# A perceiver block with a state-space layer: the skip term of y by ScalarE instead of TensorE, and a sixth product by C on GpSimd in seven of eight steps

## The chip, the cores and the metric

The kernel runs on one core of one Trainium2 chip. The metric is the device time of one execution in microseconds (us), lower is better. The engines are named as in the profile: PE is TensorE's matmul, PEld its weight load, DVE VectorE, ACT ScalarE, POOL GpSimd, SP SyncE.

## The reference

Three layers work on x (16 sequences of 128 tokens of 512 features): cross attention to 2048 context tokens, a state-space (Mamba) block with an MLP, and a mixture of experts. The change lies in the state-space layer alone:

```python
xz = jnp.einsum('bld,ed->ble', Z, in_proj_w)
x, z = jnp.split(xz, 2, axis=-1)
x = jax.nn.silu(_causal_dw_conv(x, conv_w, conv_b))
x_dbl = jnp.einsum('bld,ed->ble', x, x_proj_w)
dt, Bm, Cm = jnp.split(x_dbl, [DTR, DTR + DS], axis=-1)
dt = jax.nn.softplus(jnp.einsum('blr,dr->bld', dt, dt_proj_w) + dt_proj_b)
A = -jnp.exp(A_log)
deltaA = jnp.exp(dt[..., None] * A)
deltaBx = dt[..., None] * Bm[:, :, None, :] * x[..., None]
# over l: h = deltaA * h + deltaBx;  y = sum over the 16 states of h * C
y = ys.transpose(1, 0, 2) + x * D
y = y * jax.nn.silu(z)
return jnp.einsum('bld,ed->ble', y, out_proj_w)
```

The inner width is 1024 (8 chunks of 128 channels on the partitions) and there are 16 states. `x * D` is the skip term.

## The kernel before

The program has three stages, attention, state space (`mamba`) and MLP with experts. Each engine has its own instruction list, written by hand, and semaphores order the engines.

**Steps, pairs, units.** The state space takes 8 steps (`i` = 0 to 7) of two sequences each, 256 tokens. A step has 4 pairs of chunks and for each pair 8 groups of two states: 32 units, `m` = 0 to 31, with `p = m // 8` and `g = m % 8`. All five engines walk over the same units, each at its own place:

- POOL multiplies `dt_u` by B into one of four slots of `drive` (L1009). It waits until PE has summed unit m - 4, which held the slot.
- ACT makes the decay factors, a copy of zeros (L1163) and four `Exp` of 254 elements (L1167), in one of two PSUM slots of `decay`. It waits for the product by C of unit m - 2, or for its scan alone where that product is POOL's.
- DVE scans (L1299), then multiplies by C into `drive` (L1310). For units in `POOL_C`, the scan writes `drive` and POOL does the multiplication (`c_product`, L981) after its own drive of unit m + 2.
- PE adds `drive` into the bank `y_ps` by two matmuls with the identity (L1444), each printed as two records.

**Ends of a pair.** When all 8 units of a pair are summed, DVE multiplies `y_ps` by the gate (`end_pair`, L1261, placed after the scan of the next pair's first unit) and signals `y_ready`. Before, PE then starts the next pair in the same bank with the skip term: two matmuls of the diagonal of D (`d_diag`, made once by POOL) by `u` (L1440).

**The next step in between.** The front work of step i + 1 is spread over the units of step i. PE: `project_heads` (L1341) after units 0 and 2, `project_out` of pair 3 of the step before after unit 3, `turn` after 6, `project_in_x` (L1356) after 8, 9, 10, 12, `project_in_z` (L1356) after 13, 14, 15, 17, 22, 23, 25, 26, `project_x` (L1382) after 16, `project_dt` (L1394) after 18 and 21, `project_out` (L1405) after 27, 29, 31. DVE: `add_heads` (L1221) after units 2 and 4, whose moments POOL's `norm_rstd` takes after its drive of unit 5, and `convolve` (L1235) after 11, 12, 13, 15. ACT: `log` (L1128) after unit 1, `silu_gate` (L1094) after 4, `silu_u` (L1084) after 17, `take_z` (L1089) after 18, 20, 26, 29, `take_dbc` (L1100, L1101, of `project_x`'s result) after 19. `silu_u`, `log` and `silu_gate` need another activation table, so a table load stands before each and before the next `Exp`.

Step numbers, unit numbers and line numbers below are those of this kernel.

Of the kernel before, what the change touches and what calls it, by code (L numbers as in the profile page):

```python
# [10 lines left out]
ALU = mybir.AluOpType  # L11
ACT = mybir.ActivationFunctionType
AX = mybir.AxisListType

P = 128
# [26 lines left out]
def cross_attention(nc, x, wq_t, bq, ctx_t, wk_t, wv_t, bk, bv, bo, q_dram, attn_dram, x_dram, heads, semaphores):  # L42

    batches, width, keys = ctx_t.shape
    chunks = width // P
# [6 lines left out]
    scale = float(hd) ** -0.5  # L52
# [12 lines left out]
    T = group * queries  # L65
    assert q_steps == 4 and x.shape == (batches, queries, width)

    with ExitStack() as ctx:
# [20 lines left out]
        ident = sb("a_ident", [P, P])  # L89
# [42 lines left out]
        attn_ready, attn_stored = sem("attn_ready"), sem("attn_stored")  # L132
# [341 lines left out]
        def run_tensor(pe):  # L474
# [197 lines left out]
                values(batches - 1, tiles - 1)  # L672
                sum_over_keys(batches - 1)

            def attention_done(eng):
                eng.wait_ge(attn_ready, (batches + 1) * chunks)

            return values_last, attention_done

        return run_sync, run_gpsimd, run_scalar, run_vector, run_tensor  # L680


def mamba(nc, x, attn_dram, wo_t, w_in_t, conv_w, conv_b, w_x_t, w_dt_t, dt_b, a_log, d_skip,
          w_out_t, norm_w, x1_dram, zm_dram, semaphores):

    batches, seq, width = x.shape
# [25 lines left out]
    ACT_ROUND, ACT_LOG0, ACT_GATE = (24, 30), 27, 4  # L712
    ACT_FIRST_Z = (0, 1, 2)
    DVE_SUM, DVE_X1, DVE_CONV = 5, (2, 4), (11, 12, 13, 15)
    LATE_GROUPS = 3
    POOL_C, POOL_C_LAST = (10, 11, 12, 16, 19), (9, 12, 26, 28)
    C_BEHIND = 2

    bc_dram = nc.dram_tensor("bc_scratch", (steps, 2 * states, T), F32).ap()
# [1 line left out]
    with ExitStack() as ctx:  # L721
        def sb(name, shape, dt=F32):
            return ctx.enter_context(nc.sbuf_tensor(name, shape, dt))
# [4 lines left out]
        def sem(name):  # L728
            return semaphores.enter_context(nc.semaphore(name))
# [30 lines left out]
        mix = sb("b_mix", [P, group, width])  # L760
        norm_sb = sb("b_norm", [P, width])
        spare = sb("b_spare", [P, group * width])
        d_diag = sb("b_d_diag", [P, inner_chunks, P])
        w_out = sb("b_w_out", [P, inner_chunks, width])
        gate = (gate_even, sb("b_gate_odd", [P, inner_chunks, T]))

# [6 lines left out]
        decay = psum("b_decay", [P, 2, SG * 2 * T])  # L773

        ready = sem("b_ready")
        a_ready, diag_ready = sem("b_a_ready"), sem("b_diag_ready")
        wo_loaded, loaded, out_loaded = sem("b_wo_loaded"), sem("b_loaded"), sem("b_out_loaded")
        x_half_loaded, z_half_loaded = sem("b_x_half_loaded"), sem("b_z_half_loaded")
        attn_loaded, x_loaded = sem("b_attn_loaded"), sem("b_x_loaded")
# [153 lines left out]
        def run_gpsimd(pool, in_last_step):  # L933
# [57 lines left out]

            def front(j, par):
                norm_rstd(j)
                pool.wait_ge(loaded, LOADED)
                pool.wait_ge(x_product, 1)
                pool.tensor_tensor(d_diag[:], ident[:].unsqueeze(1).to_broadcast([P, inner_chunks, P]),
                                   d_sb[:].unsqueeze(2).to_broadcast([P, inner_chunks, P]),
                                   ALU.mult).then_inc(diag_ready, 1)

            def body(i, par, first, last):  # L1000
                j = i + 1
# [34 lines left out]
            run_steps(pool, front, body, lambda: None)  # L1036
            return lambda: weigh_out(steps - 1)

        def run_scalar(act, in_last_step):
            act.wait_ge(ready, 7)  # L1040

            def take_squares(t):
# [82 lines left out]
            def log(j, h):  # L1125

                act.wait_ge(low_ready, j * 2 + h + 1)
                act.activation(e_round[h], e_round[h], ACT.Ln, bias=1.0).then_inc(log_ready, 1)  # L1128

            def front(j, par):  # L1130
                layernorm(j, par)
                take_turned(j)
                act.wait_ge(x_half_loaded, X_HALF_LOADED)
                for n in range(pairs):
                    tap(j, par, n)
                act.wait_ge(loaded, LOADED)
                act.activation(a_neg[:], a_neg[:], ACT.Exp).then_inc(a_ready, 1)
                silu_u(j, par)
                take_z(j, par, 0)
                take_dbc(j, True)  # L1140
                take_t(j, par, 0)
                exp_of_abs(j, 0)
                round_sum(j, 0)
                take_t(j, par, 1)
                log(j, 0)
                exp_of_abs(j, 1)
                round_sum(j, 1)
                act.wait_ge(a_ready, 2)

            def body(i, par, first, last):  # L1150
                j = i + 1
                for m in range(units):
                    p, g = m // groups, m % groups
                    if not first or m >= 2:
                        k, n = (i, m - 2) if m >= 2 else (i - 1, units + m - 2)
                        if n in on_pool(k):
                            act.wait_ge(scanned, k * units + n + 1)
                        else:
                            wait_for_c_product(act, k, n)
                    if m % (units // 2) == 0:  # L1160
                        act.wait_ge(dt_ready, i * 2 + p // 2 + 1)
                    slot = decay[:, m % 2].rearrange("p (q t) -> p q t", t=seq)
                    act.copy(slot[:, :, 0], zeros[:])  # L1163
                    for s in range(SG):
                        for cc in range(2):
                            c, q = 2 * p + cc, (s * 2 + cc) * group
                            ins = act.activation(slot[:, q:q + group, 1:], by_batch(dt[:, par, c, :])[:, :, 1:], ACT.Exp,  # L1167
                                                 scale=a_neg[:, c, g * SG + s:g * SG + s + 1])
                    ins.then_inc(decay_ready, 1)
                    if m == ACT_LOG1:  # L1170
                        log(i, 1)
                    if m == ACT_GATE:
                        silu_gate(i, par)
                    if first:
                        if m in ACT_FIRST_Z:
                            take_z(i, par, 1 + ACT_FIRST_Z.index(m))
                    else:
                        if m == ACT_SQUARES:
                            take_squares(i - 1)
                        if m == ACT_SCALE:  # L1180
                            scale_out(i - 1)
                    if last:
                        in_last_step(m)
                        continue
                    if m == ACT_XN:
                        layernorm(j, 1 - par)
                    if m == ACT_XN_T:
                        take_turned(j)
                    if m in ACT_TAP:
                        tap(j, 1 - par, ACT_TAP.index(m))  # L1190
                    if m == ACT_U:
                        silu_u(j, 1 - par)
                    if m == ACT_DBC:
                        take_dbc(j, False)
                    if m in ACT_ABS:
                        take_t(j, 1 - par, ACT_ABS.index(m))
                    if m in ACT_EXP:
                        exp_of_abs(j, ACT_EXP.index(m))
                    if m in ACT_ROUND:
                        round_sum(j, ACT_ROUND.index(m))  # L1200
                    if m == ACT_LOG0:
                        log(j, 0)
                    if m in ACT_Z:
                        take_z(j, 1 - par, ACT_Z.index(m))
# [120 lines left out]
            run_steps(dve, front, body, lambda: end_pair(steps - 1, 1, pairs - 1))  # L1325
            return lambda: add_input(steps - 1, 1, True)

        def run_tensor(pe, values_last, attention_done):
            pe.sem_inc(summed, 4)
            pe.wait_ge(ready, 7)  # L1330
            pe.wait_ge(wo_loaded, WO_LOADED)
# [78 lines left out]
            def front(j, par):  # L1410
                for b in range(group):
                    project_heads(j, b, True)
                values_last()
                turn(j, par)
                pe.wait_ge(x_half_loaded, X_HALF_LOADED)
                for n in range(pairs):
                    project_in_x(j, n)
                pe.wait_ge(z_half_loaded, Z_HALF_LOADED)
                for cc in range(2):
                    project_in_z(j, 0, cc)  # L1420
                pe.wait_ge(loaded, LOADED)
                project_x(j, par)
                for h in range(2):
                    project_dt(j, h)
                for n in range(1, pairs):
                    for cc in range(2):
                        project_in_z(j, n, cc)
                pe.wait_ge(diag_ready, 1)
                attention_done(pe)

            def body(i, par, first, last):
                j = i + 1
                for m in range(units):
                    p, g = m // groups, m % groups
                    if g == 0:

                        pe.wait_ge(y_ready, i * pairs + p + 1)
                        for cc in range(2):
                            c = 2 * p + cc
                            pe.matmul(y_ps[:, cc * T:(cc + 1) * T], d_diag[:, c], u[:, par, c, :],  # L1440
                                      start=(cc == 0), stop=False, skip_group_check=True)
                    wait_for_c_product(pe, i, m)
                    for s in range(SG):
                        ins = pe.matmul(y_ps[:], ident[:], drive[:, m % 4, s].rearrange("p c t -> p (c t)"),  # L1444
# [586 lines left out]
def perceiver_layer(nc, i, out):  # L2031
# [8 lines left out]
    with ExitStack() as semaphores:  # L2040
# [24 lines left out]
        @block.scalar  # L2065
        def _(act):
            attention[2](act)
            take_last_squares, scale_last = state_space[2](act, lambda m: high_w1(act, m))
            mlp[2](act, take_last_squares, scale_last)

        @block.vector
# [4 lines left out]

        @block.tensor
        def _(pe):
            values_last, attention_done = attention[4](pe)
            project_last_out, sum_added = state_space[4](pe, values_last, attention_done)  # L2080
            mlp[4](pe, project_last_out, sum_added)


# [34 lines left out]
```

## Time and profile before

| | |
|---|---|
| median of 3 runs | 3999.93 us (3994.23 to 4001.72) |
| the profiled execution's own time | 3999.69 us |
| its span, first to last instruction | 3997.6 us |
| state-space steps 0 to 6, all engines together | about 2475 to 3357 us |
| last step | 3357 to 3484 us |
| busy over the span | PE 3833.1 (96%), DVE 2815.2 (70%), ACT 1751.8 (44%), POOL 1285.3 (32%) |
| mean granted TensorE clock | 0.991 |

Shares over the whole span average three stages with different limits. What the change is worth is to be read between 2475 and 3484 us. "Idle before" with an arrow in a row names what the engine waited for.

### The profile page before, as it was taken

The page shows a single profiled execution, that of the slowest core. Times are in us where ns is not written, and L with a number is a line of the kernel's source. Part 1 is how long each engine was busy: PE and PEld are TensorE (multiplying, and loading weights), DVE is VectorE, ACT ScalarE, POOL GpSimd, SP SyncE. Part 2 cuts the span into 40 slices and gives each one's busy share as a digit, 9 for nine tenths or more (in the row PEclk, how much of TensorE's full clock was granted, in tenths as well). Part 3 has the DMA queues.
Part 4 walks back from the last instruction along what each step waited for, and adds up shares of the span by engine and source line. Part 5 has one row for each costly group of instructions (what it writes and reads, how often), then busy time and mean ns, then how long its engine had stood idle before and what let it go on. Part 6 is the DMA issues. An engine that isn't in the chain of part 4 may idle for free.

```text
span 3997.6 us, 83589 instructions
## 1 busy us (share of the span) xinstructions
PE 3833.1 (96%) x34880; PEld 2809.5 (70%) x34880; DVE 2815.2 (70%) x2964; ACT 1751.8 (44%) x3490; POOL 1285.3 (32%) x604
## 2 busy tenths in 40 slices
PE   8999999999999999999999998999999998799998
PEld 6777777777877777777777776555455554388886
DVE  5667667667657667667666756999999999855443
ACT  2324324424414423423433435777777778422221
POOL 1111111111011011011111112888888888821011
PEclk9999999999999999999999998999999999999999
DMA  4110110110110011010011023112211122120000
GB/s 155 38 43 29 39 43 29 39 43 29 38 53 31 29 51 31 29 51 31 29 51 40 33 67 101 33 37 64 59 59 34 42 64 85 37 77 22 32 23 21
DMA packets 96902, 183.73 MB, mean 46 GB/s; under 512 B 8450, under 2 KB 12930, under 8 KB 96547
## 3 DMA queue, kind: packets, MB, share of 16 engines
q1 hardware_dynamic: 96546, 178.27, 13.9%
q8 instruction: 311, 5.10, 0.5%
q14 instruction: 45, 0.36, 0.0%
HBM read 152.82 MB, written 25.43 MB: 45 GB/s over the span
## 4 chain that ended last, share of the span: by engine, by line
PE 78%; DVE 10%; POOL 5%; ACT 3%; issue 3%; DMA 0%; DVEq 0%; POOLq 0%; ACTq 0%; SPq 0%
PE scores L523 31%; PE scores L602 8%; PE o_acc L616 6%; PE b_y L1444 6%; PE c_acc L1961 4%; PE c_ring L1946 4%; DVE max_parts L407 4%; DVE b_decay L1299 3%; PE scores L596 3%; POOL b_drive L1009 2%; PE b_work L1356 2%; PE scores L571 2%; PE b_work L1405 2%; PE c_experts_ps L1993 1%; PE b_work L1341 1%
## 5 line engine op out<-in xcount | busy, mean ns | idle before, releaser
L244 POOL TENSOR_TENSOR c_lo<-c_raw,c_hi 128x2048 fp32r<-128x2048 f32 x64 | 294.9, 4607 | 1974.5 <-DVE c_hi L346 1974.5
L434 DVE TENSOR_TENSOR prob_sums<-prob_sums,probs 128x1024 f32<-128x1024 f32 x480 | 566.7, 1222 | 115.3 <-ACT probs L319 115.3
L1009 POOL TENSOR_TENSOR b_drive<-b_dt_u,b_bc 128x1024 f32<-128x1024 f32 x256 | 600.0, 2357 | 112.8 <-PE b_y L1444 79.0
L407 DVE TENSOR_REDUCE max_parts<-scores 128x2 f32<-128x1024 f32 x512 | 602.0, 1218 | 40.6 <-PE scores L571 40.6
L319 ACT ACTIVATE probs<-scores 128x512 f32<-128x512 f32 x1024 | 528.9, 604 | 215.3 <-PE scores L602 213.8
L399 DVE SCALAR_TENSOR_TENSOR k_lo<-scores,bk_sb,k_hi 128x512 fp32r<-128x512 f32 x256 | 192.3, 751 | 565.5 <-ACT k_hi L304 565.5
L1444 PE MATMUL b_y<-b_drive,b_ident 128*128 128x512 f32 x1024 | 497.0, 615 | 73.2 <-DVE b_drive L1310 51.9
L1299 DVE TENSOR_TENSOR_SCAN b_decay<-b_decay,b_drive 128x1024 f32<-128x1024 f32 x217 | 496.5, 2288 | 12.9 <-ACT b_decay L1167 9.2
L304 ACT ACTIVATE k_hi<-scores,bk_sb 128x512 fp32r<-128x512 f32 x256 | 176.3, 689 | 604.7 <-PE scores L523 604.7
L312 ACT COPY v_sb<-scores 128x512 f32<-128x512 f32 x240 | 140.8, 587 | 669.1 <-PE scores L523 669.1
L1167 ACT ACTIVATE b_decay<-b_dt,b_a 128x254 f32<-128x254 f32 x1024 | 425.1, 461 | 0.4
L1444 PEld LDWEIGHTS b_y<-b_drive,b_ident 128*128 128x128 f32 x1024 | 188.5, 193 | 300.3 <-issue 162.6
L602 PE MATMUL scores<-q_hi,k_lo 32*128 32x128 f32 x4096 | 304.4, 270 | 0.6 <-issue 0.6
L602 PE MATMUL scores<-q_lo,k_hi 32*128 32x128 f32 x4096 | 304.3, 270 | 0.0
L602 PE MATMUL scores<-q_hi,k_hi 32*128 32x128 f32 x4096 | 290.9, 256 | 0.0
L523 PE MATMUL scores<-c_hi,wk_hi 128*128 128x512 f32 x1024 | 287.7, 403 | 0.0
L523 PE MATMUL scores<-wv_hi,c_hi 128*128 128x512 f32 x960 | 281.5, 415 | 0.0
L616 PE MATMUL o_acc<-probs,v_sb 128*32 128x128 f32 x8192 | 277.0, 276 | 0.0
L523 PE MATMUL scores<-c_hi,wk_lo 128*128 128x512 f32 x1024 | 274.9, 390 | 0.0
L523 PE MATMUL scores<-c_lo,wk_hi 128*128 128x512 f32 x1024 | 273.8, 389 | 0.0
L1310 DVE TENSOR_TENSOR b_drive<-b_decay,b_bc 128x1024 f32<-128x1024 f32 x217 | 265.4, 1223 | 6.7
L523 PE MATMUL scores<-wv_lo,c_hi 128*128 128x512 f32 x960 | 258.7, 391 | 0.0
(231 smaller groups left out, 6506.3 us busy)
## 6 DMA issues: line engine op xcount, KB each, us to landing
c_raw<-in_ctx SPq DMA_DIRECT2D x64, 1024.0 KB, 5.2
b_bc<-bc_scratch SPq DMA_DIRECT2D x128, 256.0 KB, 4.3
c_w_raw<-in_mlp_w SPq DMA_DIRECT2D x16, 512.0 KB, 3.6
q_scratch<-v_sb SPq DMA_DIRECT2D x4, 1024.0 KB, 4.3
q_raw<-q_scratch SPq DMA_DIRECT2D x16, 256.0 KB, 5.1
q_raw<-in_x SPq DMA_DIRECT2D x16, 256.0 KB, 2.7
x_scratch<-q_raw SPq DMA_DIRECT2D x16, 256.0 KB, 5.8
attn_scratch<-attn_out_sb SPq DMA_DIRECT2D x16, 256.0 KB, 2.0
```

Source lines behind the costliest of these rows:

```text
L244: pool.tensor_tensor(c_lo[:, slot], c_raw[:], c_hi[:, slot].bitcast(F32), ALU.subtract).then_inc(c_lo_ready, 1)
L319: act.activation(probs[:, (2 * t + j // 2) % 4, j % 2, :], score_bank(t, j), ACT.Exp, scale=scale).then_inc(exp_done, 1)
L407: dve.tensor_reduce(max_parts[:, g, 2 * pair:2 * pair + 2, s], max_banks[:, 2 * pair:2 * pair + 2, :], AX.X, ALU.max).then_inc(max_taken, 1)
L434: dve.tensor_tensor(part, part, probs[:, u % 4], ALU.add).then_inc(summed, 1)
L523: ins = pe.matmul(out, lhs, rhs, start=(m == 0), stop=(m == len(steps) - 1))
L602: ins = pe.matmul(banks[j][:, g * queries:(g + 1) * queries], k_part[head_rows(j), g, ts], q_part[head_rows(j), g, :], start=False, stop=last,
L616: ins = pe.matmul(o_acc[head_rows(j), g * queries:(g + 1) * queries], v_sb[:, t, h * hd:(h + 1) * hd], probs[:, (2 * t + j // 2) % 4, j % ...
L1009: pool.tensor_tensor(drive[:, m % 4], dt_u[:, 2 * p:2 * p + 2, :].unsqueeze(1).to_broadcast([P, SG, 2, T]), bc[:, g, 0].unsqueeze(2).to_br ...
L1167: ins = act.activation(slot[:, q:q + group, 1:], by_batch(dt[:, par, c, :])[:, :, 1:], ACT.Exp, scale=a_neg[:, c, g * SG + s:g * SG + s + 1])
L1299: dve.tensor_tensor_scan(state, decay[:, m % 2], increments, 0.0, ALU.mult, ALU.add).then_inc(scanned, 1)
L1310: dve.tensor_tensor(drive[:, m % 4], decay[:, m % 2].rearrange("p (n c t) -> p n c t", c=2, t=T), bc[:, g, 1].unsqueeze(2).to_broadcast([P ...
L1444: ins = pe.matmul(y_ps[:], ident[:], drive[:, m % 4, s].rearrange("p c t -> p (c t)"), start=False, stop=(g == groups - 1 and s == SG - 1) ...
```

## The change

PE's two matmuls of D's diagonal go, with `d_diag`, its making on POOL and its semaphore. ACT writes `u * D` into `y_ps` itself: `begin_sums`, two activations (`Copy`, scale by a column of D) of 256 elements, ahead of the decay factors of units 2, 10, 19 and 26 (2, 10, 18, 26 in the last step). It waits for `y_ready`, and PE's first sum of a pair waits for it (`y_begun`). The wait for the end of the attention's use of that bank moves from PE to ACT. Unit 14 joins POOL's products by C in steps 0 to 6.

```diff
-    POOL_C, POOL_C_LAST = (10, 11, 12, 16, 19), (9, 12, 26, 28)
+    Y_BEGIN, Y_BEGIN_LAST = (2, 10, 19, 26), (2, 10, 18, 26)
+    POOL_C, POOL_C_LAST = (10, 11, 12, 14, 16, 19), (9, 12, 26, 28)
...
-                pool.wait_ge(loaded, LOADED)
-                pool.wait_ge(x_product, 1)
-                pool.tensor_tensor(d_diag[:], ident[:].unsqueeze(1).to_broadcast([P, inner_chunks, P]),
-                                   d_sb[:].unsqueeze(2).to_broadcast([P, inner_chunks, P]),
-                                   ALU.mult).then_inc(diag_ready, 1)
...
+            def begin_sums(i, par, p):
+
+                act.wait_ge(y_ready, i * pairs + p + 1)
+                for cc in range(2):
+                    c = 2 * p + cc
+                    ins = act.activation(y_ps[:, cc * T:(cc + 1) * T], u[:, par, c, :], ACT.Copy, scale=d_sb[:, c:c + 1])
+                ins.then_inc(y_begun, 1)
...
                     p, g = m // groups, m % groups
+                    if m in (Y_BEGIN_LAST if last else Y_BEGIN):
+                        if first and m == Y_BEGIN[0]:
+                            attention_done(act)
+                        begin_sums(i, par, p)
...
                     if g == 0:
-
-                        pe.wait_ge(y_ready, i * pairs + p + 1)
-                        for cc in range(2):
-                            c = 2 * p + cc
-                            pe.matmul(y_ps[:, cc * T:(cc + 1) * T], d_diag[:, c], u[:, par, c, :],
-                                      start=(cc == 0), stop=False, skip_group_check=True)
+                        pe.wait_ge(y_begun, i * pairs + p + 1)
```

ACT in step 3, from the decay factors of unit 17 to those of unit 19. Before, L1084 is `silu_u`, L1089 `take_z`, L1163 and L1167 the decay factors:

```order
L1167 ACTIVATE b_decay<-b_dt,b_a 128x2x127 x4
L1084 ACT_TABLE_LOAD
L1084 ACTIVATE b_u<-b_u 128x1024 x2
L1163 COPY b_decay<-b_zeros 128x8
L1167 ACT_TABLE_LOAD
L1167 ACTIVATE b_decay<-b_dt,b_a 128x2x127 x4
L1089 COPY b_gate_even<-b_work 128x512
L1163 COPY b_decay<-b_zeros 128x8
L1167 ACTIVATE b_decay<-b_dt,b_a 128x2x127 x4
```

The same place in the changed kernel, where L1079 is `silu_u`, L1084 `take_z`, L1130 `begin_sums`:

```order
L1174 ACTIVATE b_decay<-b_dt,b_a 128x2x127 x4
L1079 ACT_TABLE_LOAD
L1079 ACTIVATE b_u<-b_u 128x1024 x2
L1170 COPY b_decay<-b_zeros 128x8
L1174 ACT_TABLE_LOAD
L1174 ACTIVATE b_decay<-b_dt,b_a 128x2x127 x4
L1084 COPY b_gate_even<-b_work 128x512
L1130 ACTIVATE b_y<-b_u,b_d 128x256 x2
L1170 COPY b_decay<-b_zeros 128x8
L1174 ACTIVATE b_decay<-b_dt,b_a 128x2x127 x4
```

`begin_sums` of pair 2 stands behind both table loads, the factors of unit 18 and `take_z`.

ACT at the start of step 3, from the factors of unit 1 to those of unit 2, in the changed kernel (L1123 is `log`; before, the row of L1130 is not there):

```order
L1174 ACTIVATE b_decay<-b_dt,b_a 128x2x127 x4
L1123 ACT_TABLE_LOAD
L1123 ACTIVATE b_spare<-b_spare 128x1024
L1130 ACTIVATE b_y<-b_u,b_d 128x256 x2
L1170 COPY b_decay<-b_zeros 128x8
L1174 ACT_TABLE_LOAD
L1174 ACTIVATE b_decay<-b_dt,b_a 128x2x127 x4
```

Here it stands between `log` and the factors of unit 2.

POOL in step 3 from the drive of unit 14 to that of unit 21, changed kernel (L1004 makes the drives, L1009 before):

```order
L1004 TENSOR_TENSOR b_drive<-b_dt_u,b_bc 128x1024
L981 TENSOR_TENSOR b_drive<-b_drive,b_bc 128x1024
L1004 TENSOR_TENSOR b_drive<-b_dt_u,b_bc 128x1024 x2
L981 TENSOR_TENSOR b_drive<-b_drive,b_bc 128x1024
L1004 TENSOR_TENSOR b_drive<-b_dt_u,b_bc 128x1024 x2
L981 TENSOR_TENSOR b_drive<-b_drive,b_bc 128x1024
L1004 TENSOR_TENSOR b_drive<-b_dt_u,b_bc 128x1024 x3
```

Before, the four drives of units 15 to 18 stood in one row; the product of unit 14 now splits them after unit 16.

## Rows read from the trace of the kernel before

**Rows 1.** Stretches of step 3: length, then each engine's busy us, PEclk, DMA

```profile
2897.00:2913.00 16.00, 13.92 (x54) 9.60 (x53) 15.79 (x20) 11.77 (x31) 16.00 (x8) 1.00 0.09 34
2913.00:2929.00 16.00, 16.00 (x59) 11.09 (x60) 15.04 (x17) 10.91 (x22) 11.92 (x6) 1.00 0.00 0
2929.00:2955.00 26.00, 26.00 (x85) 14.51 (x84) 23.97 (x15) 20.82 (x48) 21.88 (x10) 1.00 0.01 3
```

**Rows 2.** Timeline of PE, step 3: start, length, operation, count, idle before

```profile
2912.89 1.98 PE L1444 MATMUL b_y<-b_drive,b_ident 128*128 128x512 f32 x4 [2.08 <-POOL b_drive L981]
...
2928.50 1.03 PE L1440 MATMUL b_y<-b_u,b_d_diag 128*128 128x256 f32 x4
2929.36 1.88 PE L1444 MATMUL b_y<-b_drive,b_ident 128*128 128x512 f32 x4
```

**Rows 3.** Timeline of DVE, first scan of steps 2, 3, 4 and 5

```profile
2729.26 2.29 DVE L1299 TENSOR_TENSOR_SCAN b_decay<-b_decay,b_drive 128x1024 f32<-128x1024 f32 x1
...
2856.01 2.30 DVE L1299 TENSOR_TENSOR_SCAN b_decay<-b_decay,b_drive 128x1024 f32<-128x1024 f32 x1
...
2981.17 2.30 DVE L1299 TENSOR_TENSOR_SCAN b_decay<-b_decay,b_drive 128x1024 f32<-128x1024 f32 x1
...
3106.55 2.30 DVE L1299 TENSOR_TENSOR_SCAN b_decay<-b_decay,b_drive 128x1024 f32<-128x1024 f32 x1
```

**Rows 4.** Timeline of DVE, step 3: scans 10, 11, 14, 15 and end_pair

```profile
2896.65 4.46 DVE L1299 TENSOR_TENSOR_SCAN b_drive<-b_decay,b_drive 128x1024 f32<-128x1024 f32 x2
...
2914.40 2.29 DVE L1299 TENSOR_TENSOR_SCAN b_decay<-b_decay,b_drive 128x1024 f32<-128x1024 f32 x1
...
2917.86 2.29 DVE L1299 TENSOR_TENSOR_SCAN b_decay<-b_decay,b_drive 128x1024 f32<-128x1024 f32 x1
...
2926.97 0.69 DVE L1261 TENSOR_TENSOR b_gate_odd<-b_y,b_gate_odd 128x512 f32<-128x512 f32 x1 [0.78 <-PE b_y L1444]
```

**Rows 5.** Timeline of POOL, step 3: product 12, drives 15 to 17

```profile
2910.49 2.35 POOL L981 TENSOR_TENSOR b_drive<-b_drive,b_bc 128x1024 f32<-128x1024 f32 x1
2912.80 4.67 POOL L1009 TENSOR_TENSOR b_drive<-b_dt_u,b_bc 128x1024 f32<-128x1024 f32 x2
2920.13 2.36 POOL L1009 TENSOR_TENSOR b_drive<-b_dt_u,b_bc 128x1024 f32<-128x1024 f32 x1 [2.67 <-PE b_y L1444]
```

**Rows 6.** Timeline of ACT: before unit 10, take_z, two Exp

```profile
2893.30 0.17 ACT L1163 COPY b_decay<-b_zeros 128x8 f32<-128x8 f32 x1 [1.11 <-DVE b_drive L1310]
...
2929.49 0.57 ACT L1089 COPY b_gate_even<-b_work 128x512 f32<-128x512 f32 x1
...
2999.43 0.87 ACT L1167 ACTIVATE b_decay<-b_dt,b_a 128x254 f32<-128x254 f32 x2
```

**Rows 7.** Timeline of step 4: PE's first sum of pair 2, ACT's take_z

```profile
3054.64 1.98 PE L1444 MATMUL b_y<-b_drive,b_ident 128*128 128x512 f32 x4
...
3055.46 0.58 ACT L1089 COPY b_gate_odd<-b_work 128x512 f32<-128x512 f32 x1
```

**Rows 8.** Timeline of the start of step 4: PE, ACT, DVE

```profile
2986.55 1.03 PE L1440 MATMUL b_y<-b_u,b_d_diag 128*128 128x256 f32 x4
...
2985.31 0.16 ACT L1163 COPY b_decay<-b_zeros 128x8 f32<-128x8 f32 x1
...
2986.77 1.66 ACT L1167 ACTIVATE b_decay<-b_dt,b_a 128x254 f32<-128x254 f32 x4
...
2988.56 2.29 DVE L1299 TENSOR_TENSOR_SCAN b_decay<-b_decay,b_drive 128x1024 f32<-128x1024 f32 x1
...
2992.84 0.69 DVE L1221 TENSOR_TENSOR b_x<-b_work,b_x 128x512 f32<-128x512 f32 x1 [0.73 <-PE b_work L1341]
```

**Rows 9.** Stretches around units 5 to 8: steps 3, 2, 4

```profile
2874.00:2897.00 23.00, 18.92 (x55) 9.04 (x54) 22.75 (x20) 14.78 (x40) 18.83 (x15) 1.00 0.06 24
...
2748.00:2771.00 23.00, 19.54 (x47) 9.10 (x46) 20.69 (x19) 13.81 (x37) 19.32 (x15) 0.85 0.06 24
3000.00:3023.00 23.00, 19.54 (x53) 9.24 (x52) 22.05 (x20) 13.98 (x38) 19.67 (x15) 0.93 0.06 23
```

More of the change, by code:

```diff
@@ L673, in values_last, with attention_done @@
                 sum_over_keys(batches - 1)
[L675 to L680, printed above, removed]
+            return values_last
+        def attention_done(eng):
+            eng.wait_ge(attn_ready, (batches + 1) * chunks)
+        return run_sync, run_gpsimd, run_scalar, run_vector, run_tensor, attention_done
 def mamba(nc, x, attn_dram, wo_t, w_in_t, conv_w, conv_b, w_x_t, w_dt_t, dt_b, a_log, d_skip,
@@ L762, in mamba @@
         spare = sb("b_spare", [P, group * width])
-        d_diag = sb("b_d_diag", [P, inner_chunks, P])
         w_out = sb("b_w_out", [P, inner_chunks, width])
@@ L775, in mamba @@
         ready = sem("b_ready")
-        a_ready, diag_ready = sem("b_a_ready"), sem("b_diag_ready")
+        a_ready, y_begun = sem("b_a_ready"), sem("b_y_begun")
         wo_loaded, loaded, out_loaded = sem("b_wo_loaded"), sem("b_loaded"), sem("b_out_loaded")
@@ L1037, in run_gpsimd, with run_scalar @@
             return lambda: weigh_out(steps - 1)
-        def run_scalar(act, in_last_step):
+        def run_scalar(act, in_last_step, attention_done):
             act.wait_ge(ready, 7)
@@ L1326, in run_vector, with run_tensor @@
             return lambda: add_input(steps - 1, 1, True)
-        def run_tensor(pe, values_last, attention_done):
+        def run_tensor(pe, values_last):
             pe.sem_inc(summed, 4)
@@ L1427, in front @@
                         project_in_z(j, n, cc)
-                pe.wait_ge(diag_ready, 1)
-                attention_done(pe)
             def body(i, par, first, last):
@@ L2067, in _ @@
             attention[2](act)
-            take_last_squares, scale_last = state_space[2](act, lambda m: high_w1(act, m))
+            take_last_squares, scale_last = state_space[2](act, lambda m: high_w1(act, m), attention[5])
             mlp[2](act, take_last_squares, scale_last)
@@ L2078, in _ @@
         def _(pe):
-            values_last, attention_done = attention[4](pe)
-            project_last_out, sum_added = state_space[4](pe, values_last, attention_done)
+            values_last = attention[4](pe)
+            project_last_out, sum_added = state_space[4](pe, values_last)
             mlp[4](pe, project_last_out, sum_added)
```

## The prediction

> **What bounds the kernel now.** I first read the stretches of the state space, because the change touches nothing else. No engine fills a step alone. Instead the limit walks from engine to engine, and one clean step (3) shows it. From 2897 to 2913 us POOL is busy for all 16.00 us [rows 1]: drives of units 12 to 15 and the products by C of units 10, 11, 12. PE waits 2.08 us for the last of these products and starts the sum of unit 12 at 2912.89 [rows 2]. From there PE has not a single gap: 16.00 of 16 us and 26.00 of 26 us [rows 1], to the sum of unit 23. That releases the end of pair 2 on DVE, which is then dense with scans and products into the next step, up to the moments that POOL's `norm_rstd` needs after unit 5, and POOL starts its dense run again. So a step is a ring: POOL, then PE (units 12 to 23), then DVE (24 to 31, 0 to 4). One turn takes 2981.17 - 2856.01 = 125.16 us [rows 3]. Within PE's part DVE has slack: it waits 0.78 us for PE before the end of pair 1 [rows 4].
>
> **Unit 14 on POOL.** DVE loses one product per step. Start to start, scan 14 to scan 15 is 3.46 us with the product between, and two scans without one take 4.46, so 2.23 each: 1.23 us less per step, in seven steps 8.6 us of DVE's work [rows 4]. It goes where PE bounds. DVE reaches the end of pair 1 earlier and waits 0.78 + 1.23 = 2.0 us there, since PE's sum of unit 15 comes no earlier. What does move by 1.23 us is ACT: the factors of unit 17 wait for the product of unit 15, and behind them stand `silu_u`, the factors of unit 18 and `take_z`. POOL's added product takes 2.35 us (that of unit 12) and fits: the drive of unit 16 ends at 2917.47, the product at 2919.8, and the drive of unit 17 cannot start before 2920.13 anyway, held back 2.67 us by PE's sum of unit 13 [rows 5]. PE itself reaches unit 14 only after that sum and one more projection. Cost nothing; without that gap it would be up to 2.35 us per step.
>
> **The skip term on ACT: its price.** Before shows no scaled copy from SBUF into PSUM. The nearest row is two `Exp` of 254 elements, SBUF to PSUM with a scale by a column, 0.87 us together [rows 6]. Bounds: below, nothing (a write could hide in the gap); above, two of 512 elements as in `take_z`, 0.57 each, 1.14 us [rows 6]. I take 0.87.
>
> **Pair 2, the place that decides.** Before, PE starts the diagonal at 2928.50 and the first sum at 2929.36, 0.86 us [rows 2]. Now PE is free at 2928.50 and waits for `begin_sums`, which stands behind `take_z`. In step 3: `take_z` started at 2929.49, now 1.23 earlier; plus its 0.57 and 0.87 for `begin_sums` gives 2929.70. `y_ready` is not what holds it: the end of pair 1 runs from 2926.97 for 0.69 [rows 4]. So the sum of unit 16 is 0.34 us later than before, not 0.86 earlier. Behind it on PE stand `project_x`, whose result ACT takes ahead of the factors of unit 20, and all sums to unit 23, gap free: the ring gets 0.34 longer. In step 4 PE's sum started at 3054.64 and `take_z` at 3055.46 [rows 7]: 3055.46 - 1.23 + 0.58 + 0.87 = 3055.68, 1.04 later. The same sum over each step gives about 1.0 for steps 0, 2, 4, 5 and 0.3 for 1, 3, 6: 4 x 1.04 + 3 x 0.34 = +5.2 us.
>
> **Pair 0.** PE comes straight from `project_out`, starts the diagonal at 2986.55 and would have its bank ready in time, since ACT is free for `begin_sums` at 2985.31 and done at 2986.18 [rows 8]. PE gains 0.86 us, and the heads come 0.86 earlier. But the factors of unit 2 end at 2988.43 + 0.87 = 2989.30, so scan 2 slips from 2988.56 by 0.74 [rows 8]. DVE had waited 0.73 us for the heads at 2992.84 [rows 8], and this wait goes. The two cancel: 0 in steps 1 to 6. In step 0 PE's queue is late and DVE waits much longer for the heads, so there the 0.86 is gained: -0.9. In the last step no heads stand behind scan 2, and 0.74 stays: +0.7.
>
> **Pairs 1 and 3, and the rest.** Before unit 10 of step 3 ACT idles 1.11 us for DVE's product, which covers 0.87, and before unit 26 longer [rows 6]; PE's sum waits for the same product. Pair 1 lies in POOL's part, pair 3 in DVE's: 0. With that cover gone it would be 0.87 each. The diagonal's making on POOL stood in a long idle stretch before step 0, and the wait for the attention's end has long been met: 0.
>
> **Sum.** 5.2 - 0.9 + 0.7 = +5.0 us on the execution's own 3999.7 us, which is 0.2 us below the median of the three runs: **4005 us**, +0.12%. That is inside what a measurement of this kernel can tell from no change, 0.2% or 8 us.
>
> **Rivals.**
>
> *A, DVE is the bound (faster).* DVE is busy for 15.79 of 16 and 15.04 of 16 us [rows 1], so one can argue that each product less is 1.23 us less. It holds if PE's part gives way too, that is if `begin_sums` is ready before PE is free at 2928.50: then PE also sheds its 0.86 per step. 7 x 1.23 = 8.6, and 0.9 in step 0: 3990 us. Against it: `take_z` alone ends about 2928.8 in step 3 and 3054.8 in step 4, after PE is free. For it: I replayed only two steps, and a shift of ACT by half a microsecond more turns each +1.0 into +0.5.
>
> *B, the clock (slower).* PE idles in units 5 to 8, busy for 18.92 of 23 us in step 3 at the full 2.4 GHz [rows 9]. In steps 2 and 4 the same stretch shows 0.85 and 0.93 of it, so part ran at 1.2 GHz [rows 9]. The price: step 2 took 2856.01 - 2729.26 = 126.75, step 4 3106.55 - 2981.17 = 125.38, against 125.16 [rows 3], 1.59 and 0.22 us. The change takes matmuls out just before and after this stretch, 0.86 us each. And a slow stretch delays DVE, hence `take_z`, hence pair 2 (the 1.04 against the 0.34). If steps 1, 3, 6 each get a short slow piece: 3 x (0.22 + 0.70) = 2.8, 4007.8 us, the point from which it decides. If all seven get a long one: 3 x (1.59 + 0.70) + 3 x 1.37 = 11.0, 4016 us.
> The Trainium skill has this as a rule that speaks against the change: in "TensorE: Matmul & The Clock Gate", section "HAM oscillation — how this bites in real kernels", idle gaps between bursts of matmuls can send the clock back to half rate. The trace agrees in kind (2.67 us waits, levels above), and by the rule alone rival B would be likelier than I make it.
>
> *C, the write is dearer or ends later for PE.* With 1.14 instead of 0.87, pair 2 gets +0.27 in seven steps and the last step +0.27: 4007 us. With half of it, 0.44: -0.43 x 7, 4002. Both count as no change.
>
> *D, the change does not do what it says.* PE's time falls by 8 short matmuls per step but PE's ring is not shorter; that is my forecast's own case.
>
> **Numbers.** Forecast with C and the lower half of B: 0.62, range of its own 3998 to 4008. A in full: 0.18. B beyond 4007.7, or stalls of this kind that I did not find: 0.20. So faster by over 0.2% 0.18, within 0.62, slower 0.20. Range 3990 to 4014: A's end below, most of B above; about 0.15 lies outside.
>
> **What would show it.** In the profile of the changed kernel: PE waits for ACT's L1130 in front of the first sum of pair 2, about 1 us in every step and up to 2; DVE waits about 2 us for PE before the end of pair 1 and no less than before at the end of pair 2; POOL's drive of unit 17 starts as late after unit 16 as before; a short wait of DVE for ACT before scan 2 and none for the heads. Steps of 125.4 to 126.5 us. I am wrong if PE does not wait for L1130 (then A), if slow clock pieces appear in nearly every step (B), or if steps fall below 124.5 us.

## The result, and the profile after

| | before | changed |
|---|---|---|
| median of 16 runs each | 3998.14 us | 4005.72 us |
| ratio, 95% interval | | 1.0020 (1.0012 to 1.0028) |
| profiled execution's own time, span | 3999.69, 3997.6 us | 4009.79, 4008.0 us |
| mean granted TensorE clock | 0.991 | 0.986 |

The change costs 7.6 us. One execution of the changed kernel, at 5348.59 us with a mean clock of 0.65, is left out of the ratio. The profiled execution of the changed kernel lies 4 us above its median, so sizes below are taken per step, not from the span.

The busy times of the changed kernel's page, each engine's us, share of the span and instructions:

```profile
PE 3817.6 (95%) x34752; PEld 2790.9 (70%) x34752; DVE 2807.4 (70%) x2957; ACT 1779.9 (44%) x3554; POOL 1300.3 (32%) x610
```

PE lost 15.5 us of work and DVE 7.8, ACT gained 28.1 and POOL 15.0. The two engines that the change relieves are two of the three that take turns in setting the length of a step, and still the kernel is slower. The timeline of step 3 shows where. PE first (start us, length us, operation, count, idle before), the rows that answer to [rows 2]:

```profile
2928.55 1.88 PE L1444 MATMUL b_y<-b_drive,b_ident 128*128 128x512 f32 x4
2930.26 1.89 PE L1363 MATMUL b_work<-b_xn_t,b_w_in 128*128 128x256 f32 x8
2933.87 1.98 PE L1444 MATMUL b_y<-b_drive,b_ident 128*128 128x512 f32 x4 [1.72 <-ACT b_y L1130]
2935.78 3.67 PE L1389 MATMUL b_work<-b_u,b_w_x 128*64 128x256 f32 x16
```

ACT in the same place, from the factors of unit 17 to those of unit 18 and what follows, the rows that answer to [rows 6]:

```profile
2924.52 1.66 ACT L1174 ACTIVATE b_decay<-b_dt,b_a 128x254 f32<-128x254 f32 x4
2926.20 1.28 ACT L1079 ACT_TABLE_LOAD   x1
2927.50 2.01 ACT L1079 ACTIVATE b_u<-b_u 128x1024 f32<-128x1024 f32 x2
2929.41 0.16 ACT L1170 COPY b_decay<-b_zeros 128x8 f32<-128x8 f32 x1
2929.57 1.28 ACT L1174 ACT_TABLE_LOAD   x1
2930.87 1.67 ACT L1174 ACTIVATE b_decay<-b_dt,b_a 128x254 f32<-128x254 f32 x4
2932.47 0.58 ACT L1084 COPY b_gate_even<-b_work 128x512 f32<-128x512 f32 x1
2932.95 0.87 ACT L1130 ACTIVATE b_y<-b_u,b_d 128x256 f32<-128x256 f32 x2
```

ACT is busy without a gap from the factors of unit 17 to the end of `begin_sums` at 2933.82, and PE starts 0.05 us later. Before, PE had no wait at this place in step 3. What the step pays shows in the next projection, `project_x`, from whose start PE is without a gap up to the sum of unit 23. Before, it stood here:

```profile
2931.17 3.67 PE L1382 MATMUL b_work<-b_u,b_w_x 128*64 128x256 f32 x16
```

That is 2931.17 - 2856.01 = 75.16 us after the step's first scan; in the changed kernel it is 2935.78 - 2859.58 = 76.20. The 1.04 us between them is the whole difference of the two steps (125.16 and 126.20 us).

DVE and POOL between units 14 and 20, the rows that answer to [rows 4] and [rows 5]:

```profile
2918.65 2.28 DVE L1306 TENSOR_TENSOR_SCAN b_drive<-b_decay,b_drive 128x1024 f32<-128x1024 f32 x1
2920.85 2.27 DVE L1306 TENSOR_TENSOR_SCAN b_decay<-b_decay,b_drive 128x1024 f32<-128x1024 f32 x1
...
2930.46 0.69 DVE L1268 TENSOR_TENSOR b_gate_odd<-b_y,b_gate_odd 128x512 f32<-128x512 f32 x1 [1.30 <-PE b_y L1444]
...
2941.92 2.30 DVE L1306 TENSOR_TENSOR_SCAN b_decay<-b_decay,b_drive 128x1024 f32<-128x1024 f32 x1 [1.65 <-ACT b_decay L1174]
```

```profile
2921.01 2.35 POOL L981 TENSOR_TENSOR b_drive<-b_drive,b_bc 128x1024 f32<-128x1024 f32 x1
2923.62 2.37 POOL L1004 TENSOR_TENSOR b_drive<-b_dt_u,b_bc 128x1024 f32<-128x1024 f32 x1 [0.25 <-PE b_y L1444]
```

Scan 15 follows scan 14 after 2.20 us, where 3.46 lay between them. DVE then gives the gain back in two waits: 1.30 us for PE before the end of pair 1, and 1.65 us for ACT before scan 20, whose factors stand behind `take_dbc` and so behind PE's late `project_x`. POOL's added product fits its gap, and the drive of unit 17 still waits 0.25 us for PE.

The second loss shows in the stretches around units 5 to 8 (length, busy us of PE, PEld, DVE, ACT, POOL, granted clock, DMA share, GB/s), which answer to [rows 9]. They are those of steps 1 to 6 of the changed kernel:

```profile
2623.00:2646.00 23.00, 16.96 (x42) 7.40 (x41) 22.75 (x20) 15.67 (x40) 18.58 (x15) 0.95 0.06 24
2751.00:2774.00 23.00, 17.57 (x45) 7.77 (x44) 22.15 (x19) 15.79 (x40) 18.50 (x15) 0.93 0.06 23
2878.00:2901.00 23.00, 17.58 (x46) 8.06 (x46) 22.07 (x20) 14.93 (x39) 19.36 (x15) 0.93 0.06 23
3004.00:3027.00 23.00, 17.57 (x46) 7.98 (x45) 22.05 (x19) 15.15 (x39) 19.15 (x15) 0.93 0.06 24
3130.00:3153.00 23.00, 17.57 (x45) 7.81 (x44) 22.05 (x19) 15.37 (x40) 18.91 (x15) 0.93 0.07 24
3256.00:3279.00 23.00, 17.58 (x44) 7.76 (x43) 22.05 (x19) 15.60 (x40) 18.68 (x15) 0.93 0.06 23
```

All six steps have a piece at 1.2 GHz here. Before, three of the six had one. Where it stands, PE's sums take longer (3.66 us instead of 1.98 for one of them in step 3), the end of pair 0 is late, and DVE is 0.7 us late from unit 9 on. Step 3 went from 125.16 us to 2985.78 - 2859.58 = 126.20, step 4 from 125.38 to 126.25. The steps 2 to 6 take 126.14 to 126.25 us; step 1, 128.08, has a second slow piece while PE waits for `begin_sums`.

### The profile page after: what moved, and what is told of

Its sections match the earlier page's. It is cut to its first block and busy times, and to the rows that moved or that the text cites. A ratio compares the mean times of both kernels' runs of the same rounds, so it can differ in the third digit from the quotient of the medians.

```text
span 4008.0 us, 83427 instructions
## 1 busy us (share of the span) xinstructions
PE 3817.6 (95%) x34752; PEld 2790.9 (70%) x34752; DVE 2807.4 (70%) x2957; ACT 1779.9 (44%) x3554; POOL 1300.3 (32%) x610
## 5 line engine op out<-in xcount | busy, mean ns | idle before, releaser
L1004 POOL TENSOR_TENSOR b_drive<-b_dt_u,b_bc 128x1024 f32<-128x1024 f32 x256 | 600.4, 2359 | 123.6 <-PE b_y L1444 77.6
L1444 PE MATMUL b_y<-b_drive,b_ident 128*128 128x512 f32 x1024 | 507.6, 626 | 106.3 <-DVE b_drive L1317 74.6
L1306 DVE TENSOR_TENSOR_SCAN b_decay<-b_decay,b_drive 128x1024 f32<-128x1024 f32 x210 | 480.5, 2288 | 28.5 <-ACT b_decay L1174 20.9
L1317 DVE TENSOR_TENSOR b_drive<-b_decay,b_bc 128x1024 f32<-128x1024 f32 x210 | 256.9, 1223 | 6.4
```

Of the source, the lines that this page charges most:

```text
L1004: pool.tensor_tensor(drive[:, m % 4], dt_u[:, 2 * p:2 * p + 2, :].unsqueeze(1).to_broadcast([P, SG, 2, T]), bc[:, g, 0].unsqueeze(2).to_br ...
L1306: dve.tensor_tensor_scan(state, decay[:, m % 2], increments, 0.0, ALU.mult, ALU.add).then_inc(scanned, 1)
L1317: dve.tensor_tensor(drive[:, m % 4], decay[:, m % 2].rearrange("p (n c t) -> p n c t", c=2, t=T), bc[:, g, 1].unsqueeze(2).to_broadcast([P ...
```

## The experiments

Each kernel was timed against the kernel before on the same chip. "Steps" are distances between first scans of successive steps in the profile.

### Unit 14 on GpSimd alone

The edit to the kernel before:

```diff
-    POOL_C, POOL_C_LAST = (10, 11, 12, 16, 19), (9, 12, 26, 28)
+    POOL_C, POOL_C_LAST = (10, 11, 12, 14, 16, 19), (9, 12, 26, 28)
```

> The kernel before with one edit: the product by C of unit 14 moves to GpSimd, the skip term stays on TensorE. Times are against the kernel before. Theory 1 (the late begin_sums of pair 2 is the loss, everything else of the change is hidden): DVE reaches the end of pair 1 earlier and waits there, so hardly any gain; only steps 0 and 2, where TensorE waited for unit 16's product, can gain up to 1 us each: -3 to 0 us. Rival A (DVE is the bound): -8.6 us. Rival D (GpSimd has no room for a sixth product): up to 7 x 2.35 = +16 us, and TensorE waits longer for products of GpSimd than the 21.2 us before.

Measured: 3998.43 us against 3999.48, ratio 0.9997 (0.9988 to 1.0006). Steps 1 to 6 take 125.15 to 125.20 us, though four of these six have a slow clock piece: the spread of before (125.15 to 126.75) is gone, the floor of 125.15 is not. (The 126.75 of before had a piece twice as long, and none of these six steps has one of that length.) So one product less on DVE in every step does not shorten the ring while PE's part of it stays as long. That rules out rival A for this kernel, and rival D.

### begin_sums on ScalarE alone

The edit to the changed kernel:

```diff
-    POOL_C, POOL_C_LAST = (10, 11, 12, 14, 16, 19), (9, 12, 26, 28)
+    POOL_C, POOL_C_LAST = (10, 11, 12, 16, 19), (9, 12, 26, 28)
```

> The changed kernel with one edit: unit 14's product stays on DVE, begin_sums on ScalarE. Against the kernel before. Theory 1: the factors of unit 17, silu_u, take_z and with them begin_sums of pair 2 come 1.2 us later than in the changed kernel, in seven steps 8.6 us on top of its 7.6: +13 to +17 us, TensorE's wait for L1130 grows by about 1.2 us a step. Rival D (the sixth product on GpSimd costs the time): +2 us or less, faster than the changed kernel. Rival B (the clock alone): about +8, no difference from the changed kernel.

Measured: 4018.67 us, ratio 1.0048 (1.0034 to 1.0061), +19.2 us, a little over the range given. The timeline of PE in step 3:

```profile
2933.44 1.89 PE L1363 MATMUL b_work<-b_xn_t,b_w_in 128*128 128x256 f32 x8
2938.56 3.43 PE L1444 MATMUL b_y<-b_drive,b_ident 128*128 128x512 f32 x4 [3.23 <-ACT b_y L1130]
```

The wait is 3.23 us instead of 1.72. The sum behind it takes 3.43 us instead of 1.98: the clock has fallen to 1.2 GHz in the wait. Steps alternate between 126.7 and 129.3 us. Those of 129.3 have two slow pieces, one around unit 9 and this one; those of 126.7 have none. The second piece accounts for what the expectation lacked.

### Pair 2's skip term back on TensorE

The edit to the changed kernel; `d_diag` and its making on POOL are back as well:

```diff
-    Y_BEGIN, Y_BEGIN_LAST = (2, 10, 19, 26), (2, 10, 18, 26)
+    Y_BEGIN, Y_BEGIN_LAST = (2, 10, 26), (2, 10, 26)
...
+                    if g == 0 and p == 2:
+                        pe.wait_ge(diag_ready, 1)
+                        pe.wait_ge(y_ready, i * pairs + p + 1)
...
+                    elif g == 0:
+                        pe.wait_ge(y_begun, i * (pairs - 1) + (p if p < 2 else p - 1) + 1)
```

> The changed kernel, but pair 2's skip term is TensorE's again (two matmuls with the diagonal), pairs 0, 1 and 3 stay on ScalarE. Against the kernel before. Theory 1: TensorE starts the sum of unit 16 about 1.0 us earlier than in the changed kernel, 7 us in seven steps, and the second slow clock stretch of step 1 goes too: -2 to +1.5 us, steps of about 125.3 us. Rival B (the loss is the slow clock around units 5 to 8, which stays here): +5 us or more. Rival E (the loss is scan 2 slipping behind begin_sums of pair 0): no better than the changed kernel, +6 to +8.

Measured: 3997.09 us against 3999.48, ratio 0.9992 (0.9983 to 1.0002). Steps 1 to 6 take 125.02 to 125.07 us. The place is shown: with pair 2's skip term alone put back, the loss of 7.6 us is gone. Most steps have their slow clock piece around units 5 to 8 here too, and it costs nothing, since DVE has slack again before the end of pair 1. So rival B as a loss by itself falls, and so does rival E, that scan 2 slipping behind `begin_sums` of pair 0 is the loss.

### TensorE's gaps filled

The edit to the changed kernel:

```diff
                     ins.then_inc(summed, 1)
+                    if not last and m in (5, 7):
+                        pe.wait_ge(x1_ready, (j + 1) * group)
+                        for _ in range(5 if m == 5 else 4):
+                            pe.matmul(work[:, 2, 0:T], wo[:, 0, 0:P], wo[:, 0, 0:T], start=True, stop=True)
```

> The changed kernel plus matmuls whose result is not used, in TensorE's gaps: 5 of 256 columns behind the sum of unit 5 and 4 behind that of unit 7, steps 0 to 6, into a bank that is free there. They take 0.43 us each and so fit the gaps of 2.67 and 2.0 us. Against the kernel before. Rival B in its mild form (each step's slow clock stretch delays DVE by 0.7 us and that delays begin_sums): the granted clock is 1.00 around units 5 to 8, steps fall from 126.2 to about 125.4: 0 to +3 us. Theory 1 without any part of the clock: +7 to +9 us, no change from the changed kernel.

Measured: 4004.99 us against 3999.48, ratio 1.0013 (1.0004 to 1.0022): +5.5, between the two expectations. Stretches of steps 1 to 3: around units 5 to 8, then 31 us later, around units 12 to 16:

```profile
2621.00:2644.00 23.00, 20.86 (x66) 11.37 (x65) 22.75 (x20) 15.63 (x41) 18.67 (x15) 1.00 0.06 24
2747.00:2770.00 23.00, 20.85 (x68) 11.65 (x67) 22.75 (x20) 15.66 (x42) 19.28 (x15) 1.00 0.06 24
2873.00:2896.00 23.00, 20.86 (x66) 11.46 (x66) 22.75 (x20) 15.64 (x42) 18.95 (x15) 1.00 0.06 24
```

```profile
2652.00:2675.00 23.00, 20.94 (x76) 13.99 (x75) 20.61 (x27) 17.81 (x41) 21.56 (x10) 1.00 0.06 24
2778.00:2801.00 23.00, 20.93 (x69) 13.43 (x68) 19.26 (x25) 16.91 (x38) 19.90 (x10) 0.93 0.06 23
2904.00:2927.00 23.00, 20.93 (x70) 13.46 (x69) 19.60 (x25) 16.91 (x37) 19.90 (x10) 0.93 0.06 23
```

The filling did its work where it stands, 1.00 in every step. But in steps 2 to 6 a slow piece stands around units 12 to 16 instead, and those steps stayed at 126.3 us. It does its harm in another way there: it lies on PE's own gap-free part, where the sum of unit 12 takes 3.68 us instead of 1.98 (step 2), and PE then has hardly a wait left for `begin_sums` (0.14 us).

```profile
2785.50 3.68 PE L1444 MATMUL b_y<-b_drive,b_ident 128*128 128x512 f32 x4 [2.07 <-POOL b_drive L981]
```

Step 1 has none in either place, and it takes 125.40 us (first scans at 2603.28 and 2728.67):

```profile
2603.28 2.29 DVE L1306 TENSOR_TENSOR_SCAN b_decay<-b_decay,b_drive 128x1024 f32<-128x1024 f32 x1
...
2728.67 2.30 DVE L1306 TENSOR_TENSOR_SCAN b_decay<-b_decay,b_drive 128x1024 f32<-128x1024 f32 x1
```

That step splits the loss. Without a slow piece the changed kernel's ring is 125.40 - 125.16 = 0.24 us longer than before; a slow piece adds 0.8 to 0.9. It is one step alone, but the second experiment agrees with it: its three steps without a slow piece take 126.67 to 126.68 us, 1.27 more, where unit 14 on DVE is worth 1.23.

### begin_sums of pair 2 ahead of unit 18

The edit to the changed kernel:

```diff
-    Y_BEGIN, Y_BEGIN_LAST = (2, 10, 19, 26), (2, 10, 18, 26)
+    Y_BEGIN, Y_BEGIN_LAST = (2, 10, 18, 26), (2, 10, 18, 26)
```

> The changed kernel with one number changed: begin_sums of pair 2 stands ahead of the factors of unit 18 (behind silu_u) in steps 0 to 6, not ahead of those of unit 19. Against the kernel before. Theory 1: ScalarE reaches it about 3 us earlier and then waits for y_ready; TensorE's sum of unit 16 starts about 1.2 us sooner than in the changed kernel, the factors of unit 18 slip by up to 3 us, which DVE can bear as far as it had waited for TensorE before the end of pair 2: -3 to +1 us, if that slack holds. Rival F (the slip of unit 18's factors takes the place of the wait): +6 us or more, DVE waits over 1.5 us a step for ScalarE before scan 18. Rival B (the clock alone): +7 as the changed kernel.

Measured: 3992.35 us against 3999.84, ratio 0.9982 (0.9973 to 0.9991): -7.5 us, faster than both kernels and 4.5 us better than the low end of what was expected. ACT, PE and DVE in step 3:

```profile
2919.69 2.00 ACT L1079 ACTIVATE b_u<-b_u 128x1024 f32<-128x1024 f32 x2
2923.37 0.87 ACT L1130 ACTIVATE b_y<-b_u,b_d 128x256 f32<-128x256 f32 x2 [1.68 <-DVE b_gate_odd L1268]
...
2922.45 1.89 PE L1363 MATMUL b_work<-b_xn_t,b_w_in 128*128 128x256 f32 x8
2924.30 1.98 PE L1444 MATMUL b_y<-b_drive,b_ident 128*128 128x512 f32 x4
...
2927.33 2.30 DVE L1306 TENSOR_TENSOR_SCAN b_decay<-b_decay,b_drive 128x1024 f32<-128x1024 f32 x1 [0.53 <-ACT b_decay L1174]
```

`begin_sums` ends at 2924.24 and PE goes on from `project_in_z` almost without a gap: it sheds the diagonal's 0.86 us at last. The slipped factors of unit 18 cost DVE 0.53 us, inside its slack, so rival F, that this slip takes the place of the wait, falls. Steps 1 to 6 take 124.39 to 124.43 us, 0.76 less than before, with or without a slow clock piece (two of the six have none). The expectation was too small on both counts: it had the sum of unit 16 start 1.2 us sooner than in the changed kernel, where step 3 shows it 2924.30 - 2851.78 = 72.52 us after the first scan, not 2933.87 - 2859.58 = 74.29: 1.77 sooner, and it did not foresee that the slow pieces would cost nothing.

### begin_sums of pair 2 ahead of take_z

The edit to the changed kernel:

```diff
-    Y_BEGIN, Y_BEGIN_LAST = (2, 10, 19, 26), (2, 10, 18, 26)
+    Y_BEGIN, Y_BEGIN_LAST = (2, 10, 26), (2, 10, 18, 26)
...
                     ins.then_inc(decay_ready, 1)
+                    if m == 18 and not last:
+                        begin_sums(i, par, p)
```

> The changed kernel with begin_sums of pair 2 directly behind the factors of unit 18, ahead of take_z, in steps 0 to 6; nothing else moves. Against the kernel before. Theory 1: it comes earlier by take_z's spacing, 0.48 us a step, 3.4 us in seven steps: about +4 us, steps of 125.75 us against 126.2 in the changed kernel. Rivals B and E (clock, or pair 0): no difference from the changed kernel, +7 to +8 us.

Measured: 4001.67 us against 3999.84, ratio 1.0004 (0.9995 to 1.0013): +1.8, 2 us better than expected. Four of steps 1 to 6 take 125.7 to 125.9 us and the other two 124.9. They are 0.5 us shorter than the changed kernel's with and without a slow piece (126.2 and 125.40; one step, at 125.9, only 0.3), as 0.48 of `take_z` wants it; the two steps without a slow piece are the rest.

### Pairs 0 and 2 on TensorE

The kernel of the third experiment with `Y_BEGIN = (10, 26)` in all steps, and the diagonal's matmuls for `p in (0, 2)`.

> The changed kernel with the skip terms of pairs 0 and 2 on TensorE, pairs 1 and 3 on ScalarE. It differs from the kernel with only pair 2 on TensorE (-2.4 us against before) in pair 0 alone. Against the kernel before. Theory 1 with pair 0 as predicted: steps 1 to 6 within 0.15 us of that kernel's 125.05, step 0 about 0.9 us longer, the last step 0.7 us shorter: -2.5 to -1.5 us. Rival E (begin_sums of pair 0 costs 0.7 us a step by scan 2): -7 to -8 us, steps of 124.4 us.

Measured: 3997.02 us against 3999.84, ratio 0.9990 (0.9981 to 0.9999): -2.8. Steps 1 to 6 take 125.17 to 125.19 us (125.02 to 125.07 with pair 0 on ACT), step 0 128.20 (126.80). Pair 0 on ScalarE is worth 0.13 us a step, 1.4 in step 0, and costs 0.7 from the first scan of the last step to its last sum. Rival E, which asked for -7 or more here, falls.

### Ahead of unit 18, without unit 14 on GpSimd

The edit to the kernel with `begin_sums` of pair 2 ahead of unit 18:

```diff
-    POOL_C, POOL_C_LAST = (10, 11, 12, 14, 16, 19), (9, 12, 26, 28)
+    POOL_C, POOL_C_LAST = (10, 11, 12, 16, 19), (9, 12, 26, 28)
```

> The kernel with begin_sums of pair 2 ahead of unit 18, and unit 14's product back on DVE. Against the kernel before. Theory 1 now says that unit 14 on GpSimd pays only by making ScalarE earlier ahead of begin_sums of pair 2. Here ScalarE waited 1.68 us for y_ready in that place, more than the 1.23 us that unit 14 shifts it, so nothing is lost: -8 to -6 us, steps of 124.4 to 124.6 us. Rival A (DVE's work counts): +8.6 us on top of -7.5, so about +1 us.

Measured: 3998.05 us against 3998.84, ratio 0.9997 (0.9988 to 1.0006): -0.8, not -8 to -6. The expectation of the time was wrong. Its expectation of the step was right for a step with the full clock: the two of steps 1 to 6 without a slow piece take 124.52 and 124.53 us, inside the 124.4 to 124.6 expected. The four with one take 125.33 to 125.52, while with unit 14 on POOL such a step cost nothing extra (124.39 to 124.43). Step 3 is one of these four; PE and POOL in it:

```profile
2926.81 1.96 PE L1444 MATMUL b_y<-b_drive,b_ident 128*128 128x512 f32 x4 [1.09 <-POOL b_drive L981]
...
2924.32 2.35 POOL L981 TENSOR_TENSOR b_drive<-b_drive,b_bc 128x1024 f32<-128x1024 f32 x1 [1.32 <-DVE b_drive L1306]
```

The slow piece has made DVE late, and the sum of unit 16 waits for unit 16's own product on POOL, and that for scan 16 on DVE. The same sum in step 1, without a slow piece, has no such wait:

```profile
2675.98 1.95 PE L1444 MATMUL b_y<-b_drive,b_ident 128*128 128x512 f32 x4
```

In step 0 PE waits 2.32 us for this product (1.04 with unit 14 on POOL), and the step takes 128.14 us instead of 127.01. Unit 14 on POOL brings scan 16 1.23 us forward. So it has two uses, one for `begin_sums` and one as slack ahead of unit 16 when DVE is late, and the second was missed.

### The changed kernel once more

No edit.

> The changed kernel once more, unaltered, with a second profile. Against the kernel before. If its slow clock stretch around units 5 to 8 belongs to the kernel, it is there again in nearly every step of this profile, steps of 126.2 us, and the time is +5 to +9 us. If it was chance, some steps are without it and take 125.4 us, as the one such step of the filled kernel did.

Measured: 4005.68 us against 3998.84, ratio 1.0015 (1.0006 to 1.0024). Steps 1 to 6 take 126.08 to 126.20 us, each with a slow piece around units 5 to 8. It belongs to this kernel's schedule, not to one profile. The second slow piece is not in step 1 this time but in step 0, which takes 131.47 us (130.01 in the first profile).

## Why the prediction was right, point by point

**The time.** 4005 us was forecast, 4005.72 came. Against the kernel before, 5.0 us were forecast and 7.6 measured, so part of the agreement is the 1.8 us by which the 16-run median of before lies under the first three runs. That part is luck. The forecast's own range was 3998 to 4008 us. The timing of the last experiment gives 6.8 us for the same two kernels, so the cost is 7 to 8 us.

**The ring.** Right for steps with the full clock. Shown by unit 14 alone on POOL (1.23 us less DVE work a step, 125.15 us as before) and by pair 2 alone (all of the loss).

**Pair 2 decides.** Right in place and in sign. PE waits for L1130 in front of the first sum of pair 2. The sum starts 2933.87 - 2859.58 = 74.29 us after the step's first scan, against 2929.36 - 2856.01 = 73.35: 0.94 late in step 3, where 0.34 was forecast, and 0.86 in step 4, where 1.04 was. `begin_sums` took the 0.87 us that the two `Exp` of 254 elements had suggested. Without a slow piece the ring is 0.24 us longer than before. Against the kernel with pair 2 alone on PE it is 125.40 - 125.05 = 0.35 us longer, where the forecast had 0.34 for this place.

What was mis-sized is the slow clock pieces. The sum left the clock as it was in each step of before, while the changed kernel has a piece in every one. Of the steps forecast at +0.34, step 3 came at +1.04, step 6 at +1.05 and step 1 at +2.93 (+0.93 in the second profile). Step 2 was forecast at +1.04 and came at 126.14 - 126.75 = -0.61: its long slow piece of before, 0.85 in [rows 9], did not return, and PE had waited there 0.72 us for POOL's product of unit 16, which the forecast did not see. Steps 0 to 6 together were forecast at +4.3 and came at +6.8 and +6.1 in the two profiles. So some of the errors cancelled.

**Rival B.** Its mild form is part of what happened, priced at 2.8 us on top of 5.0: 7.8 forecast, 7.6 measured. The prediction named slow pieces in nearly every step as a sign that it is wrong. By that sign this rival came true, at the very edge from which it was said to decide, and the forecast of the time held since its mild form costs so little. The long form, 11 us, did not come. As the prediction said, the slow piece costs by making DVE late, hence `take_z`, hence pair 2. Step 1 of the filled kernel and the kernel with pair 2 on PE show both halves: without the slow piece 125.40 us, and with a slow piece but without ACT's gate 125.05. That fewer matmuls around units 5 to 8 cause the piece is supported by PE's busy time there (18.92 us of 23 before in the undisturbed steps, 17.57 after, 20.86 filled) and is not shown by more than that: with the place filled, a piece stood elsewhere in the step.

**Pair 0.** Right in its mechanism. Scan 2 stood 2867.68 - 2859.58 = 8.10 us after the first scan, before 7.39: 0.71 late, 0.74 forecast. DVE's wait for the heads is gone and scan 3 comes 0.10 us earlier than before. The first scan of the last step to its last sum took 0.75 us longer, where 0.74 was forecast. The profile puts DVE's wait of 0.62 us before scan 2 in step 3 down to POOL's drive and not to ACT. But before, the same row of three drives ended at 2864.07, after scan 2 had started at 2863.40, so it is not what scan 2 needs; the factors of unit 2 end at 2867.65 and the scan starts at 2867.68. The two effects did not quite cancel in the inner steps: pair 0 on ScalarE is worth 0.13 us a step and 1.4 in step 0, where 0 and 0.9 were forecast.

**Unit 14 on POOL.** Its cost, nothing, was right. DVE's wait for PE before the end of pair 1 was forecast at 2.0 us; it is 1.30 in step 3, where the slow piece takes the rest, and 2.11 in the filled kernel's step without one. Its worth was told only in part: without it the change costs 19.2 us and not 7.6, and the version ahead of unit 18 gains 0.8 and not 7.5.

**Rival A.** Its condition was that `begin_sums` is ready before PE is free. One number in the order of ScalarE nearly meets it: ahead of unit 18 the kernel takes 3992.35 us, close to A's 3990. The prediction took 19 as the place, as the change has it, and never asked what 18 would do in the inner steps.

**Open.** The rest of the 2.6 us between forecast and result is not settled to the microsecond. The time from the last step's first scan to the end was 643.5 us in the changed kernel's first profile and 641.3 in its second, 640.5 before. Behind the last sum of the state space the profiles fall into two groups, whatever the kernel: 521.1 us before, in the second profile of the changed kernel and in two of the experiments, 523.0 to 524.1 in the others. So 2.3 us of the first profile do not come from the change. Why the changed kernel has a slow piece in every step, and the kernel before in three of six, stays open too.

## What to carry to other kernels

When the limit walks round several engines, replay one turn row by row: work taken from a busy engine pays only in its own part of the ring. Work moved to an idle engine is not free if that engine reaches it late; what counts is what stands ahead of it in the queue, here two table loads, and a place one unit earlier turned 7.6 us of loss into 7.5 of gain. Keep slack ahead of a wait that repeats, since it also absorbs slow clock pieces: without unit 14 on POOL the same place gained 0.8 us.

## What the runs showed of the hardware

A piece at 1.2 GHz can come back at the same place of every step, 126.3 us after the last one where the step takes 126.3. With matmuls put into its place the clock was 1.00 there, and in five of six steps a piece stood about 27 us later in the step. PE's busy time does not tell why it stood there: the stretch was as busy in a step with the piece (20.93 of 23 us, 0.93 of the clock) as in the one without (20.94, 1.00), and part of the 20.93 is matmuls that ran at half the clock.

The price of a piece depended on the slack behind it. It was 0.8 to 0.9 us a step in the changed kernel, 0.2 in two steps of before, and nothing that can be seen (125.02 to 125.07 us, 124.39 to 124.43) where DVE had slack. One piece of before, twice as long, cost 1.59. A wait of 3.23 us of PE was followed by a sum of 3.43 us instead of 1.98, at half the clock.
